# Values of the cross-attention tile by tile, with a column of ones that sums the probabilities

## The reference

```python
x = _layernorm(x + _L0_attn_ref(x, Wq, Wk, Wv))              # 16 heads of 16, 1024 keys, no mask
x = _layernorm(x + _L0_xattn_ref(x, ctx, ctx, mask, ...))    # 16 heads of 16, 77 keys, masked
x = _layernorm(x + _L0_ffn_ref(x, ...))                      # 8 experts of 512, the top 2 per token
```

```python
energy = jnp.einsum('bhqd,bhkd->bhqk', Q, K) * scale
energy = jnp.where(m == 0, -1000000000.0, energy)
attn = jax.nn.softmax(energy, axis=-1)
out = jnp.einsum('bhqk,bhkd->bhqd', attn, V)
out = out.transpose(0, 2, 1, 3).reshape(B, S, HID)
return out @ Wo + bo
```

## Time and profile before

| | us |
|---|---|
| median of 3 runs (852.06 to 857.89) | 855.1 |
| the profiled execution, its own time | 856.25 |
| its span in the trace | 854.4 |
| busy: TensorE, VectorE, ScalarE, GpSimd | 713.2, 639.0, 487.8, 305.5 |
| mean granted TensorE clock | 0.924 |

### The profile page before, as it was taken

How to read it: one execution, slowest core, us unless ns; L and a number is a source line. 1 busy time by engine, 2 the same in 40 slices (tenths; PEclk the granted TensorE clock), 3 DMA queues, 4 the chain that set the end, 5 groups by cost and what they waited for, 6 DMA issues and landing times.

```text
span 854.4 us, 14878 instructions
## 1 busy us (share of the span) xinstructions
PE 713.2 (83%) x4760; PEld 332.1 (39%) x4760; DVE 639.0 (75%) x1087; ACT 487.8 (57%) x982; POOL 305.5 (36%) x249
## 2 busy tenths in 40 slices
PE   6789999999999999999998868867679888789800
PEld 3442222223222222222222235545367566667600
DVE  3487888877888888887875689999737446689765
ACT  2225677777777677776777554342436566457622
POOL 8000600000000398881002575666712554444411
PEclk9898999999999999999999888887679999899965
DMA  7746040030400689883000090000241333412121
GB/s 196 187 110 148 16 93 21 19 75 20 94 20 25 155 239 278 260 253 125 2 1 1 1 380 14 1 2 7 75 124 52 100 105 90 143 53 90 58 99 49
DMA packets 51171, 80.75 MB, mean 95 GB/s; under 512 B 16468, under 2 KB 35415, under 8 KB 49689
## 3 DMA queue, kind: packets, MB, share of 16 engines
q1 hardware_dynamic: 37065, 44.91, 19.2%
q0 software_dynamic: 9952, 31.29, 11.8%
q10 hardware_dynamic: 4080, 3.61, 1.7%
HBM read 48.21 MB, written 33.11 MB: 95 GB/s over the span
## 4 chain that ended last, share of the span: by engine, by line
PE 54%; DVE 26%; DMA 6%; issue 5%; ACT 4%; POOL 2%; SPq 1%; DVEq 1%; another core or an unknown queue 1%; ACTq 0%; POOLq 0%
PE bank L544 12%; PE bank L536 12%; PE quad L517 11%; DVE rowmax L959 6%; PE quad L868 6%; PE bank L885 5%; DMA kstack<-k_parts 3%; PE bank L468 2%; DVE hl L1189 2%; DVE sc L1062 2%; ACT probs L1495 2%; DVE sum L1074 2%; DVE max L1069 2%; DMA qstack<-q_parts 1%; DVE attn_all L1175 1%
## 5 line engine op out<-in xcount | busy, mean ns | idle before, releaser
L959 DVE TENSOR_REDUCE rowmax<-quad 128x1 f32<-128x1024 f32 x256 | 303.0, 1218 | 77.1 <-PE quad L517 76.5
L1495 ACT ACTIVATE probs<-bank 128x512 f32<-128x512 f32 x512 | 284.3, 595 | 115.6 <-PE bank L536 112.8
L536 PE MATMUL bank<-qstack,kstack 98*128 98x512 bf16 x512 | 195.0, 389 | 12.9 <-ACT probs L1495 11.2
L517 PE MATMUL quad<-kstack,qstack 96*128 96x512 bf16 x512 | 178.4, 388 | 15.2 <-DVE rowmax L959 6.6
L868 PE MATMUL quad<-xbT,w 128*128 128x128 bf16 x1104 | 121.1, 224 | 25.6 <-DVE hl L1189 16.0
L544 PE MATMUL bank<-probs,v_all 128*32 128x512 f32 x1024 | 140.3, 617 | 0.0
L536 PEld LDWEIGHTS bank<-qstack,kstack 98*128 98x128 bf16 x512 | 49.0, 97 | 193.9 <-ACT probs L1495 163.2
L868 PEld LDWEIGHTS quad<-xbT,w 128*128 x1104 | 91.3, 100 | 58.5 <-issue 43.3
L1619 ACT ACTIVATE hid<-quad,b 128x128 f32<-128x128 f32 x184 | 52.6, 369 | 65.1 <-PE quad L868 49.5
L517 PEld LDWEIGHTS quad<-kstack,qstack 96*128 96x128 bf16 x512 | 48.6, 99 | 77.4 <-DVE rowmax L959 39.8
L1839 POOL DMA_INDIRECT y_tokens<-ysb,dest x46 | 47.7, 1038 | 84.1 <-DVE ysb L1203 75.3
(11 more groups left out here) (184 smaller groups left out, 951.3 us busy)
## 6 DMA issues: line engine op xcount, KB each, us to landing
xb<-x_sorted SPq DMA_DIRECT2D x46, 129.0 KB
x_sorted<-blank POOLq DMA_DIRECT2D x6, 774.0 KB, 9.1
w1raw<-in_w POOLq DMA_DIRECT2D x8, 512.0 KB, 6.1
w2raw<-in_w POOLq DMA_DIRECT2D x8, 512.0 KB, 6.3
w_split<-w1two POOLq DMA_DIRECT2D x8, 512.0 KB, 5.7
w_split<-w2two POOLq DMA_DIRECT2D x8, 512.0 KB, 4.4
w<-w_split SPq DMA_DIRECT2D x16, 256.0 KB, 5.2
w<-w_split SPq DMA_DIRECT2D x4, 1024.0 KB, 11.8
```

Of the source, the lines that this page charges most:

```text
L517: mm = pe.matmul(bank[2 * (p % 2) + e], q, kstack[slot][0:MAXROW, j, e * 512:e * 512 + 512], start=True, stop=True)
L536: mm = pe.matmul(bank[4 + i % 2], kstack[slot][0:KROWS, j, kt * P:kt * P + P], qstack[slot][0:KROWS, half, j, :], start=True, stop=True)
L959: dve.tensor_reduce(rowmax[:, k % 2, p:p + 1], quad[:, 2 * (p % 2):2 * (p % 2) + 2, :].rearrange("p a n -> p (a n)"), AX_X, ALU.max).then_ ...
L1495: act.activation(probs[:, i % PR, :], bank[4 + i % 2], ACT.Exp, scale=INV4).then_inc(probs_ready, 1)
```

## The change

- The sum over the keys comes out of the values' matmul: `vbd` has 17 columns per head (`OW`), the last holding ones where the row belongs to the head (`vone`, a new input of 40 columns, copied in by GpSimd). `sum_probs`, `divide` and `last_divide` are gone; `turn_probs` waits for the exponential alone.
- `values2(n)` runs once a tile, with the 128 turned probabilities as weights and `vbd` moving (136 columns for the first of five chunks of keys, then 51, 34, 51, 34), for both halves of the heads. Its output lies query by row in columns 308 to 443 of `quad` banks 0 and 1, beside the scores.
- `scale2(n)` on VectorE: reciprocal of the sums and one multiplication, both out of PSUM, into `o2n`. It stands first in body n. `turn_o2(g)` transposes a group's four tiles into banks 6 and 7, in body 0 of the next group, followed there by the output projection.
- New waits: `values2(n)` waits for `take(n + 2)` and `scale2(n - 1)`; `scores2(n + 3)` waits for `scale2(n)`. In every body the values stand ahead of the scores; in the second body of a group `turn_x1` and `project_q2` stand between them.
- `low_x2` goes from VectorE to GpSimd. `place(0)` and the two `rank` go to body 12, `place(0)` behind the last `take`, `last_shift`, `residual2(2)` and its moments; all of the first half's scatters follow on GpSimd.

```diff
+PT = 3
+V_HEADS = [(c * P // SC, (c * P + VROWS[c] - 1) // SC + 1) for c in range(VC)]
+OW = HD + 1
...
-        vbd = sb("vbd", [P, B, 2, VC, P])
+        vbd = sb("vbd", [P, B, 2, VC, HALF * OW])
+        vone = sb("vone", [P, VC, HALF])
...
-                    if n == NT - 2:
-                        pe.wait_ge(ranks_taken, 1)
+                    if n >= FAR:
+                        pe.wait_ge(o2_scaled, n - FAR + 1)
...
-                if n < NT - 2:
-                    pe.wait_ge(p2_done, n + 1)
-                else:
-                    pe.wait_ge(last_divided, n - NT + 3)
+                pe.wait_ge(p2_exp, n + 1)
...
+            def values2(n):
+
+                i, b = n % 4, n // 4 // 2
+                pe.wait_ge(pT_done, 3 * n + 3)
+                pe.wait_ge(s2_taken, min(n + FAR, NT))
+                if n:
+                    pe.wait_ge(o2_scaled, n)
+                for half in range(2):
+                    for c in range(VC):
+                        lo, hi = (0, HALF) if c == 0 else V_HEADS[c]
+                        mm = pe.matmul(O2[half][:, lo * OW:hi * OW], pT[0:VROWS[c], half, c, n % PT * P:n % PT * P + P],
+                                       vbd[0:VROWS[c], b, half, c, lo * OW:hi * OW], start=(c == 0), stop=(c == VC - 1), skip_group_check=True)
+                mm.then_inc(o2_ready, 1)
+
+            def turn_o2(g, tiles=range(4)):
...
+                for half in range(2):
+                    for i in tiles:
+                        tr = pe.transpose(bank[6 + half][:, i * P:i * P + P], o2n[:, i, half * P:half * P + P], ident[:, :])
...
                 if i == 1 and g < TG - 1:
-                    turn_probs(n, lambda k: [project_q2(g + 1, half) for half in range(2)] if k == 0 else None)
+                    turn_probs(n, lambda k: None)
+                    values2(n)
+                    turn_x1(g + 1)
+                    for half in range(2):
+                        project_q2(g + 1, half)
                     for half in range(2):
                         next_scores(half)
...
+                turn_probs(n, lambda k: None)
+                if i == 0 and g:
+                    turn_o2(g - 1)
+                values2(n)
+                for half in range(2):
+                    next_scores(half)
+                if i == 0 and g:
+                    project_o2(g - 1)
+                if i == 2 and 0 < g < TG - 1:
                     turn_x2(g - 1)
...
+                if n == NT - 4:
+                    rank(0)
+                    rank(1)
...
+            def scale2(n):
+
+                out = quad[:, 0:2, FREE - 12:FREE - 12 + HALF * OW].rearrange("p a (h d) -> p a h d", d=OW)
+                inv = inv2[:, n % 2, :].rearrange("p (a h) -> p a h", a=2)
+                dve.wait_ge(o2_ready, n + 1)
+                dve.reciprocal(inv, out[:, :, :, HD]).then_inc(o2_recip, 1)
+                dve.wait_ge(o2_recip, n + 1)
+                if n >= 4:
+                    dve.wait_ge(o2_turned, 2 * (n // 4))
+                dve.tensor_tensor(o2n[:, n % 4, :].rearrange("p (a h d) -> p a h d", a=2, d=HD), out[:, :, :, 0:HD],
+                                  inv.rearrange("p a (h o) -> p a h o", o=1).to_broadcast([P, 2, HALF, HD]), ALU.mult).then_inc(o2_scaled, 1)
...
+                scale2(n)
+                if i == 1 and g:
+                    root_moments(4 * g - 4, 4 * g)
+                    norm_x2(g - 1)
+                if n + FAR < NT:
+                    take(n + FAR)
```

More of the change, by code:

```diff
@@ L283, in build @@
         Y_BANK = (6, 7)
-        SCORED = (9, 13)
-        X2_BANK = (6, 6, 0)
+        SCORED = (10, 14)
+        X2_BANK = (6, 6, 2)
+        O2 = [quad[:, half, FREE - 12:FREE - 12 + HALF * OW] for half in range(2)]
         BLOCKS = 2 * HB
@@ L1055, in norm_x1, with take @@
                                       ALU.subtract, ALU.mult).then_inc(x1_done, 1)
-            def take(n, between=None):
+            def take(n):
                 dve.wait_ge(s2_ready, n + 1)
@@ L1830, in _ @@
                     root(2, KT, NT)
-            for k in range(2, HT):
+                if i == 3 and g:
+                    low_x2(g - 1)
+            for k in range(HT):
                 for j in range(2):
                     scatter(k, j)
+            low_x2(TG - 2)
             def send_block(m):
```

188 lines of the change are left out of this document (54 added, 134 removed).

## The result

| | median us | runs | from, to |
|---|---|---|---|
| before | 853.58 | 4 | 851.2, 857.89 |
| after | 896.39 | 4 | 893.57, 900.3 |

The ratio is 1.0499, with a 95% interval of 1.0431 to 1.0567: the change makes the kernel 5% slower. The profiled run took 900.3 us, span 898.5; 885 had been forecast.

The account below looks back on a forecast made before the run. VectorE was taken to bound cross-attention; the change makes a TensorE-VectorE ring whose steps add up. First experts' block +31.2 us, less 1.5 for low halves, is +29.7: 886.0 on the profiled 856.25, 884.8 on the median, called 885; range 865 to 905.

Parts of the forecast that it names:

- rival C: Cross-attention: TensorE falls to its lower clock through new pauses; values 4.5, turning 2.9 in ten bodies, +20, 905 us; 15%.
- B: Cross-attention: the ring costs less, bodies 1.5 us or more shorter; 865 us, 863 with a landing at 2 us; 10%.
- The sign of a group of 43 to 46 us: Profile after: a group of four cross-attention tiles takes 43 to 46 us; under 38 would show the forecast wrong.
- The ring: Cross-attention: values, scaling, scores and take wait for each other through banks 0 and 1; a plain body is 7.1 us.
- Rival A: Cross-attention: VectorE stays the bound, its work to the row numbers 94 us instead of 102.8; 840 us; 5%.
- The dated schedule: Cross-attention: take of tile 3 at 496.3 us, then body lengths added up to the last scores at 623.6.
- Tile 1: Second tile of a group: turning, values, x1, query projection and scores in a row, scaling hidden; 13.0 us.
- Body 8: Cross-attention: VectorE's 9.1 us, top-two included, against TensorE's 6.0; the body takes 10.8 us, to 579.8.
- The tail: End of cross-attention: row numbers at 633.9 us, sixteen scatters to 654.2, first experts' block turned at 659.3, +31.2.
- Low halves: Two groups of x2's low halves leave VectorE's cross-attention, 9 us; eight leave its experts' stage, 1.5 us.
- Rival D: GpSimd without divisions frees VectorE's normalisations, moments and `fill`; 4 to 6 us less, 880; forecast with it 70%.

Follow-up runs that it names:

- 4: Changed kernel with sixteen of a tile's twenty value records left out, so the output is not the layer's; 876.05 us, 1.0268 to the kernel before.
- experiment 5: Changed kernel with the values in a bank of their own and the turned probabilities in bank 4 alone; 934.22 us, 1.094 to the kernel before.
- 6: As experiment 5, with the scores three tiles ahead put into the pauses of turning; 912.29 us, 1.0659 to the kernel before.
- 7: Changed kernel with eight more transposes per tile, repeating done work, in TensorE's wait for the scaling; 892.56 us, 1.0402 to the kernel before.
- experiment 8: Changed kernel with the first scored group's top-two ahead of the normalising of x1 in tile 7's body; 899.55 us, 1.0502 to the kernel before.
- experiment 3: Changed kernel with ranks ahead of the last scores and row numbers ahead of the last take; 899.12 us, 1.0533 to the kernel before.
- 9: As experiment 3, with six of the sixteen scatters ahead of the root on GpSimd; 899.72 us, 1.0528 to the kernel before.
- experiment 1: Kernel before with only the low halves of x2 moved from VectorE to GpSimd; 851.84 us, 0.9972 to the kernel before.
- experiment 2: Changed kernel with the low halves back on VectorE, one body later than in the kernel before; 907.01 us, 1.0612 to the kernel before.
- 12: As experiment 11, with logits behind half the values, last scores and take earlier, seven scatters ahead of the root; 845.71 us, 0.9966 to the kernel before.
- experiment 11: Changed kernel with own bank, values a tile late, early row numbers, then four waits taken out; 870.86 us, 1.0158 to the kernel before.

## Why the prediction was right, and where it was off

The sign and the mechanism held, the size was 14 us short: 886.0 forecast on the profiled run's time, 900.3 measured. By medians the kernel became 42.8 us slower where 29.7 were forecast; 896.4 is inside the range of 865 to 905, and nearer to rival C's 905 than to the 885. The range's ends were those of rivals B and C; the terms listed for it add up to -9.5 and +21, 875 to 906. The sign of a group of 43 to 46 us failed: the two groups took 50.7 and 47.8.

- **The ring takes VectorE's place as the bound.** Right: VectorE 51% busy, 11.1 us of scores waiting for scaling. Rival A is out; its 102.8 us of work was the length of the window to the row numbers, in which VectorE was busy for 95.1. Experiments 4 to 7 put the weight on TensorE's side of the ring: turning, values and scores stand in a row, and the clock at which they run decides as much as the waits between them.
- **The dated schedule.** Take of tile 3 at 495.80 (496.3 forecast); behind body 2 519.69 (516.4); body 3 529.57 (524.6); body 4 538.15 (532.9). Bodies 5 to 7 took 35.2 us, forecast 36.1. Body 8 took 15.6 (10.8), bodies 9 to 12 47.8 (43.8). Last scores 636.6 (623.6). The 13 us fall in three places: tile 1 of the first group +4.6, body 8 +4.8, bodies 9 to 12 +4.0; the rest cancels. As identical instructions of body 5 differ by 2.7 us from one profiled kernel to the next (experiment 8), some of the +4.6 and +4.0 may be chance.
- **Tile 1, 13.0 forecast, 17.6 measured the first time.** The term mis-sized is the clock's: values 4.53 where I took 2.8, query projection 6.13 where I took 3.6. In the second group values (2.44) and query projection (3.70) met the full clock, and the body took 16.7 with the output projection, as forecast, but by luck: the output projection took 5.29 where 3.7 was put. The mean of the values was 3.3 us, between my 2.8 and rival C's 4.5; four of the twelve tiles in the window took 4.4 to 4.5, five 2.44. So rival C was half right, and my one figure for a mean clock hid that projections double as well.
- **Body 8.** The step that failed: I compared VectorE's 9.1 us with TensorE's 6.0 and gave the body 10.8. That treats the top-two as work beside the ring. `turn_o2` waits for the logits' copy before the values may start, so VectorE's 4.02 us of normalising and TensorE's values, at the lower clock after it, add up. The wait is in the code, `logits_taken` ahead of bank 6, and I had not walked that queue. Taking it away alone made the body 4.2 us shorter, though the same normalising then stands ahead of the scaling; the time of the whole did not show it (experiment 8).
- **The tail.** Right to 0.8 us in its parts: last scores to row numbers 10.5 us (10.3 forecast, with 2.4 from the ranks' copy to the row numbers; the rows it named give 4.7 less 1.7, 3.0, and 2.6 came, so the close hit is in part luck), first scatter to the end of the last 20.2 (20.3), to the load 1.6, to the first block 2.7 (3.5). That this chain alone sets the experts' start was wrong: the last tile's values end at the same time (experiments 3 and 9), which the forecast did not need but a remedy does.
- **Low halves.** I put 9 us of VectorE's time into what the change frees and 1.5 us into the experts' stage. Alone they are worth 2 us (experiment 1); inside the change they are worth about 10 (experiment 2), since there they stand ahead of what TensorE waits for. The 1.5 us in the experts' stage did not come: 226.6 us against 226.3.
- **Rival D.** Right in part. `fill` took 0.23 us, as argued. The normalising of x2 fell from 6.6 us for eight rows to 2.8, and that of x1 in body 4 took 1.38 where 3.2 was put. But the other of x1 took 4.02, beside a shift and low halves on GpSimd, and body 3's residual and statistics 4.7 where 3.6 was put. GpSimd had lost its divisions there, but kept the shift and gained the low halves.

## What to carry to other kernels

Before work is moved off a busy engine, write the new dependencies down as one cycle and add it up; if it runs through two engines and one pair of banks, the stretch becomes the sum of both. Price the steps of an engine whose clock moves at both levels, projections as well as the new form, and look for what fills its pauses: here filling them was worth more than removing the waits. Take a wait away only after reading what stands next in the same queue, and look in the profile whether the body itself became shorter: of the repairs 3, 5, 8 and 9 none made the kernel faster that the times could show, though 8 made its own body 4.2 us shorter; the version that rearranged the body and took the waits out together (12) is 5% faster than the change.

## What the runs showed of the hardware

- Repeating 1.06 us of transposes in a wait of 0.90 raised the granted clock of the stretch from 0.74 to 0.83, and a stretch with 10% more busy instructions was 6.6 us shorter. With the same idle time, 27.7 and 28.1 us, the granted clock was 0.64 in experiment 5 and 0.74 in the change. And TensorE stayed at 1.2 GHz for 18 us without waiting (experiment 11), through logits, values, turning and scores. The runs show that pauses cost clock; they do not show what else decides it.
- Turning through one bank costs 0.69 to 0.75 us of TensorE's time per piece for each copy by ScalarE, 13.8 us more than two banks in 12 tiles.
- While scatters run, copies of ScalarE whose inputs TensorE had finished came late without any releaser that the profile names: 2.52 and 1.51 us with the change, 2.54, 2.88 and 1.56 in experiment 3, 1.45 and 2.52 in 9, 1.85, 4.27 and 1.53 in 8, 1.49 and 5.34 in 5, none of 1 us or more in the profiled execution of 7. The 5.34 of experiment 5 is 5.36 at the same place in 6. The cause is open, and no run tests it.
